# Context projections in fp16, and scores and maxima of an attention kernel moved to row tiles

## The reference

```
q = heads(xq @ wq);  k = heads(ctx @ wk);  v = heads(ctx @ wv)
q, k = rope(q), rope(k)                         # block 0 only
sim  = einsum('bhnd,bhmd->bhnm', q, k) * DH ** (-0.5)
a    = softmax(sim, axis=-1)
o    = einsum('bhnm,bhmd->bhnd', a, v)
out  = o.reshape(B, N, MID) @ wo + bo
```

## Time and profile before

| | |
|---|---|
| median of 3 runs | 6510.97 us |
| profiled execution | 6507.4 us, span 6505.6 us |
| TensorE matmuls busy | 5952.5 us (91%) |
| TensorE weight loads | 3685.3 us (57%) |
| VectorE busy | 4855.0 us (75%) |
| ScalarE busy | 4164.3 us (64%) |
| GpSimd busy | 2747.3 us (42%) |
| chain that ended last | PE 63%, DVE 14%, ACT 12%, issue 6% |

### The profile page before, as it was taken

How to read it: one execution, slowest core, us unless ns; L and a number is a source line. 1 busy time by engine, 2 the same in 40 slices (tenths; PEclk the granted TensorE clock), 3 DMA queues, 4 the chain that set the end, 5 groups by cost and what they waited for, 6 DMA issues and landing times.

```text
span 6505.6 us, 154557 instructions
## 1 busy us (share of the span) xinstructions
PE 5952.5 (91%) x58376; PEld 3685.3 (57%) x58376; DVE 4855.0 (75%) x9782; ACT 4164.3 (64%) x9234; POOL 2747.3 (42%) x2358
## 2 busy tenths in 40 slices
PE   6999989989899998998989999899897999989988
PEld 4566456754466645774456664577444665457744
DVE  6887777757788777775778877777578887877756
ACT  4556686657656668665755566766575566676656
POOL 3466126740256512674025651277302655127730
PEclk9999999989999999998999999999899999999989
DMA  3111011110111101111011110111001111011100
GB/s 88 37 34 27 22 37 31 33 28 13 51 35 33 30 21 37 33 30 28 17 47 37 34 27 20 39 32 33 24 19 50 30 32 30 18 41 31 28 20 12
DMA packets 347787, 206.23 MB, mean 32 GB/s; under 512 B 165005, under 2 KB 319981, under 8 KB 346926
## 3 DMA queue, kind: packets, MB, share of 16 engines
q1 hardware_dynamic: 347054, 196.34, 11.9%
HBM read 105.18 MB, written 1.05 MB: 16 GB/s over the span
## 4 chain that ended last, share of the span: by engine, by line
PE 63%; DVE 14%; ACT 12%; issue 6%; POOL 4%; SPq 1%; DVEq 0%; DMA 0%; ACTq 0%; POOLq 0%
PE ring L1354 32%; PE scores L1354 15%; PE o_acc L1354 15%; ACT qop L1652 5%; DVE max_part L2113 3%; POOL weight_sum L1316 2%; ACT region L1652 2%; DVE o_inv L2136 2%; ACT probs L1798 2%; DVE region L2075 2%; DVE ring L2089 1%; DVE ring L2092 1%; ACT qm L1652 1%; DVE raw L2087 1%; DVE qop L2072 1%
## 5 line engine op out<-in xcount | busy, mean ns | idle before, releaser
L2113 DVE TENSOR_REDUCE max_part<-ring 128x1 f32<-128x400 f32 (+2 forms) x4608 | 2425.0, 579 | 513.0 <-PE ring L1354 478.8
L1798 ACT ACTIVATE probs<-scores 128x512 f32<-128x512 f32 (+1 forms) x3840 | 2087.9, 599 | 954.2 <-PE scores L1354 929.5
L1316 POOL TENSOR_TENSOR weight_sum<-weight_sum,probs 128x512 f32<-128x512 f32 (+1 forms) x1408 | 1786.9, 1269 | 193.9 <-ACT probs L1798 60.1
L1354 PE MATMUL o_acc<-probs,region 128*32 128x256 f32 (+2 forms) x13312 | 1327.4, 383 | 11.4 <-ACT probs L1798 5.0
L1652 ACT ACTIVATE region<-ring 64x400 f16<-64x400 f32 (+4 forms) x1744 | 817.0, 479 | 463.5 <-PE ring L1354 374.1
L1316 POOL TENSOR_TENSOR weight_sum<-probs 128x512 f32<-128x512 f32 x256 | 324.8, 1269 | 1540.9 <-PE ring L1354 1096.8
L1354 PEld LDWEIGHTS o_acc<-probs,region 128*32 128x32 f32 (+2 forms) x13312 | 637.6, 123 | 400.9 <-ACT probs L1798 139.4
L1354 PE MATMUL scores<-qop,region 128*64 128x256 f16 (+1 forms) x6400 | 811.4, 274 | 21.4 <-ACT qop L1652 14.5
L1354 PE MATMUL scores<-qop,x_cop 128*64 128x256 f16 (+1 forms) x6400 | 805.2, 272 | 0.0
L1354 PE MATMUL ring<-nk,qm 128*128 128x400 f16 (+2 forms) x2560 | 709.0, 337 | 51.5 <-DVE max_part L2113 22.4
L1354 PE MATMUL scores<-qm,nk 128*128 128x512 f16 (+1 forms) x1920 | 656.0, 389 | 57.0 <-ACT probs L1798 31.4
(11 more groups left out here) (170 smaller groups left out, 7168.0 us busy)
## 6 DMA issues: line engine op xcount, KB each, us to landing
x_cop<-region SPq DMA_DIRECT2D x256, 200.1 KB, 3.1
stage<-in_wide SPq DMA_DIRECT2D x512, 64.0 KB, 1.9
nk<-region SPq DMA_DIRECT2D x192, 100.1 KB, 2.2
stage<-in_wide SPq DMA_DIRECT2D x128, 128.0 KB, 2.5
v_stage<-in_wide SPq DMA_DIRECT2D x256, 64.0 KB, 1.9
wo_stage<-in_wide SPq DMA_DIRECT2D x32, 512.0 KB, 3.9
cop_few<-kop_few SPq DMA_DIRECT2D x256, 32.0 KB, 1.9
ff_w<-in_ff_w SPq DMA_DIRECT2D x24, 256.0 KB, 3.3
```

The source lines that it names most:

```text
L1316: pool.tensor_tensor(total, before, probs[0:rows_, (un.chunk + k) % PROBS, :], ALU.add)\
L1354: return pe.matmul(out, lhs, rhs, start=start, stop=stop, skip_group_check=True)
L1798: act.activation(to, src, ACT.Exp, scale=t.scale).then_inc(exp_done.sem, 1)
L2113: dve.tensor_reduce(dst, src, AX.X, ALU.max).then_inc(*release(one))
```

## The change

It has three parts.

1. *Context in fp16.* The transposed context is stored as a high and a low fp16 part instead of fp32 (`ctx_t`, `src_t`), the low part by VectorE. The key and value weights of the wide cross stages are split the same way, times 32, at the start of the program: ScalarE makes the high, VectorE the low part, and a DMA stores them in device memory, from where each unit loads them. The narrow cross weights are folded and split once. A projection is then three fp16 products, high by high, high by low and low by high (`in_halves`), instead of one in fp32.
2. *Row tiles.* Operands stay in the order in which the projection leaves them: head h on its own 64 (wide) or 32 (narrow) partitions. A score or maximum of one head is a matmul whose weights have 64 or 32 rows and 128 columns. Heads write to different PSUM banks. The wide scores take four products for each head (high by high, high by low, low by high, and the shift). Maxima use the high parts alone, and no longer wait for the low part. The crossed copy, its DMAs, the masks and the DMAs of the narrow self stages are gone; narrow queries, and in self attention keys, are spread over the partitions by a small matmul (`spread`). Narrow cross keys are brought by twelve DMAs of 8 partitions for a unit instead of three of 32. All of an operand goes out of PSUM in one instruction of 128 partitions.
3. *One pool.* Scores and ring share seven banks, at most four for each use; scores are issued two banks at a time (2 heads by 2 key tiles).

The planner's table is changed with it, and its tile size is now a pair (rows, columns).

```diff
-RING, SLOTS, PROBS = 4, 3, 8
+POOL_BANKS, RING, SLOTS, PROBS = 7, 4, 4, 8
...
-            return [("max", (h, None), 0) for h in range(4)] + [("shift", 0, 0)]
-        out = [("max", (h, q), k) for g in (0, 2) for q in range(QT) for k in range(len(self.kc)) for h in (g, g + 1)]
-        return out + [("shift", 0, 0)]
+            return [("spread", 0, 0), ("spread", 1, 0)] + [("max", (h, None), 0) for h in range(4)] + [("shift", 0, 0)]
+        out = [("max", (h, q), k) for q in range(QT) for k in range(len(self.kc)) for h in range(4)]
+        return [("spread", 0, 0)] + out + [("shift", 0, 0)]
...
-def columns(what):
...
+def tile_of(what):
 
     if what[0] == "pre":
-        return P
+        return P, P
     un = CHUNKS[what[1]][0] if what[0] == "scores" else UNITS[what[1]]
-    if not un.t.wide:
-        return 32 if what[0] == "values" else P
-    if what[0] == "job" and un.t.jobs[what[2]][0] == "shift":
-        return P
-    return 64
+    side = 64 if un.t.wide else 32
+    if what[0] == "scores" or what[0] == "job" and un.t.jobs[what[2]][0] == "max":
+        return side, P
+    return P, side
...
-            deps = [("DVE", ("job", n, t.jobs.index(("low", k + 1, 0)))), ("DVE", ("job", n, t.jobs.index(("low", 0, 0))))]
-            self.part("PE", "max", due, one, 0.21 if t.cross else 0.3, deps, 0.2)
+            deps = [("ACT", ("job", n, op_job(t, k + 1))), ("ACT", ("job", n, op_job(t, 0)))]
+            self.part("PE", "max", due, one, 0.1 if t.cross else 0.16, deps, 0.25)
...
+        self.part("ACT", "split", due, one, 0.4, [])
+        self.part("DVE", "split", due, one, 0.55, [("ACT", one)])
+        self.part("SP", "split", due, one, 0.6, [("DVE", one)], 4.0)
...
-                        for block_, of_k, of_q in ((1, 0, 0), (2, 1, 0), (3, 0, 1)):
-                            to = slice(32 * block_, 32 * block_ + 32)
-                            sp.dma_start(nq[to, z, :], q[part, of_q, :]).then_inc(nq_in[z].sem, 16)
-                        for block_, of_k, of_q in ((1, 0, 0), (2, 1, 0), (3, 0, 1)):
-                            to = slice(32 * block_, 32 * block_ + 32)
-                            sp.dma_start(nk[to, z, 0:un.t.keys], k[part, of_k, 0:un.t.keys]).then_inc(nk_in[z].sem, 16)
+                            wait(taken(item_of(s, u, "keys", len(un.t.kc) - 1)))
+                        k = split_of(s, u, "keys")
+                        for h in range(4):
+                            rows_of = slice(32 * un.p + 8 * h, 32 * un.p + 8 * h + 8)
+                            for l, at in ((0, 8), (1, 16), (0, 24)):
+                                sp.dma_start(nk[32 * h + at:32 * h + at + 8, z, 0:un.t.keys], k[rows_of, l, 0:un.t.keys])\
+                                    .then_inc(nk_in[z].sem, 16)
...
+            wait((mod_full, 1))
+            for k, at in enumerate((SK, SV)):
+                sp.dma_start(kv_in[7][:, :, k, :], a["wide7"][:, 0:DC, at:at + P].rearrange("g p c -> p g c"))\
+                    .then_inc(kv_loaded[1], 16)
...
-                    pool.tensor_tensor(qm[:, un.narrow_at % QM_SLOTS, :, :], nq[:, z, :].unsqueeze(1).broadcast_to([P, 4, N]),
-                                       head_mask[:, :].unsqueeze(2).broadcast_to([P, 4, N]), ALU.mult)\
-                        .then_inc(masked.sem, 1)
...
+            def in_halves(out, lhs, rhs, product):
+
+                product(out, lhs[0], rhs[0], True, False)
+                product(out, lhs[0], rhs[1], False, False)
+                return product(out, lhs[1], rhs[0], False, True)
...
-                        last = mm_64(out[:, 0:w], stage[0:t.dk, w_at, k, W_K:W_K + P], src[0:t.dk, a0:a0 + w], True, True)
+                        if t.cross:
+                            halves = k_split_of(un)
+                            last = in_halves(out[:, 0:w], [halves[:, k, l, :] for l in range(2)],
+                                             [src[:, l, a0:a0 + w] for l in range(2)], mm_64)
...
-                            last = mm_64(out[:, m * w:(m + 1) * w], qop[:, z, h, qq * P:(qq + 1) * P],
-                                      kop_of(un)[:, h, a0:a0 + w], True, True)
+                            last = mm(out[:, m * w:(m + 1) * w], qop[part, z, 0, qq * P:(qq + 1) * P],
+                                      kop_of(un)[part, 0, a0:a0 + w], True, True)
...
-                    if g >= SLOTS:
-                        old, co = chunk_before(g, SLOTS)
-                        pe.wait_ge(exp_done.sem, exp_done.at(old.n, co + 1))
-                    r = t.rows(k)
-                    out = scores[0:r, g % SLOTS, :]
-                    if t.wide:
-                        for h in range(2):
-                            mm_64(out[:, h * N:(h + 1) * N], kop_of(un)[:, h, k * P:k * P + r], qop[:, z, h, :], True, False)
-                            last = mm_64(out[:, h * N:(h + 1) * N], cop_of(un)[:, h, k * P:k * P + r], qop[:, z, 2 + h, :],
-                                      False, True)
-                    else:
-                        last = mm(out, nk[:, un.narrow_at % NK_SLOTS, k * P:k * P + r],
-                                  qm[:, un.narrow_at % QM_SLOTS, 2 * half:2 * half + 2, :], True, True)
-                    last.then_inc(scores_full.sem, 1)
+                            pe.wait_ge(*taken(("job", n, op_job(t, t.ops - 1))))
+                    for one in (g, g + 1):
+                        pe.wait_ge(*room_for_scores(one))
+                    side, nz = P // t.heads, un.narrow_at % NK_SLOTS
+                    heads = [(c % t.heads + i, score_bank(g + i)) for i in range(2)]
+                    kop = kop_of(un)
+                    for m, k in enumerate(t.tiles(c // t.heads)):
+                        r = t.rows(k)
+                        at = slice(k * P, k * P + r)
+                        if t.wide:
+                            products = [(kop[:, 0, at], qop[:, z, 0, :]), (kop[:, 0, at], qop[:, z, 1, :]),
+                                        (kop[:, 1, at], qop[:, z, 0, :]), (shift_k[:, 0:r], shift_q[:, z, :])]
+                        else:
+                            products = [(nk[:, nz, at], nq_shift[:, nz, :])]
+                        for i, (keys, queries) in enumerate(products):
+                            for h, r_out in heads:
+                                part = slice(side * h, side * h + side)
+                                last = mm(ring[0:r, r_out, m * N:(m + 1) * N], keys[part], queries[part],
+                                          i == 0, i == len(products) - 1)
+                    last.then_inc(scores_full.sem, 2)
...
-                        part = slice(64 * h, 64 * h + 64)
-                        if i == 0:
-                            for to in (slice(0, 64), slice(64, 128)):
-                                last = copy(qop[to, z, h, :], ring[part, bank(one), 0:N])
-                        else:
-                            a0, w = t.kc[i - 1]
-                            last = copy(kop_of(un)[part, h, a0:a0 + w], ring[part, bank(one), 0:w])
-                    last.then_inc(op_high.sem, 1)
+                    high, w = operand(un, i, 0)
+                    copy(high, ring[:, bank(one), 0:w]).then_inc(op_high.sem, 1)
...
+                def split_high_weights(i):
+                    s, g = SPLITS[i]
+                    if g == 0:
+                        act.wait_ge(kv_loaded[s // 7], 48 if s == 1 else 32)
+                    copy(kv_out[s][:, g, :, 0, :], kv_in[s][:, g, :, :], scale=GAIN).then_inc(kv_high, 1)
...
+                def context_low(one, j):
+
+                    _, s, u, m = one
+                    a0 = (j % 4) * BANK
+                    w = min(BANK, M - a0)
+                    to = (ctx_t if j < 4 else src_t)[:, u % 2, :, a0:a0 + w]
+                    dve.wait_ge(ctx_high.sem, ctx_high.at((s, u), j + 1 if j < 4 else 2 * j - 2))
+                    dve.tensor_tensor(to[:, 1, :], ring[0:DC, bank(one), 0:w], to[:, 0, :], ALU.subtract).then_inc(*release(one))
...
-                    kop, v = kop_of(un), ring[:, bank(made), :]
                     dve.wait_ge(op_high.sem, op_high.at(n, i + 1))
-                    for h in range(2):
-                        part, other = slice(64 * h, 64 * h + 64), slice(64 - 64 * h, 128 - 64 * h)
-                        if i == 0:
-                            last = dve.tensor_tensor(qop[part, z, 2 + h, :], v[part, 0:N], qop[part, z, h, :], ALU.subtract)
-                        else:
-                            a0, w = t.kc[i - 1]
-                            last = dve.tensor_tensor(kop[other, h, a0:a0 + w], v[part, 0:w], kop[part, h, a0:a0 + w],
-                                                     ALU.subtract)
-                    last.then_inc(*release(made))
+                    high, w = operand(un, i, 0)
+                    dve.tensor_tensor(operand(un, i, 1)[0], ring[:, bank(made), 0:w], high, ALU.subtract).then_inc(*release(made))
```

481 lines of the change are left out of this document (301 added, 180 removed).

## The result

The changed kernel takes 6238.83 us (median of 4 runs, 6222.14 to 6249.06), the kernel before beside it 6511.69: a ratio of 0.9577 (95% interval 0.9561 to 0.9593). Forecast were 6000 us, so the gain is 273 us instead of 511. The profiled execution took 6242.82 us, its span is 6241.0.

The account below looks back on a forecast made before the run. TensorE streaming bounds the wide cross stages; in narrow cross stages three engines wait in turn. Terms 4 x (-20 - 17 - 66 - 28) + 12 = -512 took 6507.4 us to 5995, say 6000; range 5790 to 6330.

Parts of the forecast that it names:

- wide stages: Wide cross stages: shorter by 20 us (rope stage) and 17 us per pair, from TensorE's stream and fewer stalls.
- context values in fp16: Wide cross value projections: three fp16 steps take 0.21 us per key tile against 0.22, no gain; better bound -11 us a stage.
- change of tile: TensorE in wide cross units: more changes of tile size at 0.10 us each, adding 23 and 15 us a stage.
- Rivals A: Score and maximum matmuls: row tiles do not run side by side; about 7080 us, 4% chance.
- B: TensorE: a change between row and column tiles costs more than 0.10 us; at 0.3, 6930 us; 6% chance.
- C: Wide cross stages: short fp16 products cost 0.11 us each and maxima find no overlap; about 6290 us, 15% chance.
- Overlap of the maxima: Wide cross units: neighbouring maxima of different heads run side by side, -12 and -15 us a stage; lower bound of gain 0.
- stalls: Wide cross stages: a third of TensorE's stalls of 35 and 25 us goes, -11 and -7 us.
- Self stages: Self attention per pair: stage 6 -11, stage 0 -6, stages 3 and 9 -5 and -6; together -28 us.
- The start: Program start: sixteen weight splits on ScalarE delay the first query copy from 35.14 to near 53 us; +12 us once.
- Narrow cross: Narrow cross stages: TensorE falls to 122 us, VectorE bounds at some 90% busy; 160 and 167 us, -33 each per pair.
- rival D: Narrow cross stages: engines keep waiting in turn, -11 instead of -33 us a stage; 6176 us, 15% chance.

Follow-up runs that it names:

- kernel with two products: Changed kernel with the last of the three fp16 products left out in the wide cross key and value projections; 6051.15 us, 0.9289 of before.
- experiments 1 to 3: Changed kernel with added narrow cross matmuls (6217.9, 6197.3, 6244.0 us); with masked full-array narrow scores and maxima (6216.89, 6301.89); with those over 128 rows, unmasked (6143.15).
- kernel with whole rows: Changed kernel, same order and copies, with narrow cross scores and maxima over all 128 rows instead of 32, head mask left out; 6143.15 us, 0.9434 of before.

## Why the prediction was right and wrong

*The sum.* The time lies within the forecast's range of 5790 to 6330 us, and that is partly luck. Over the four pairs the wide cross stages gave -244 us (forecast -148), the self stages with the start -158 (forecast -100), and the narrow cross stages +134 (forecast -264). With the first two as forecast, the failed third would have put the kernel near 6390, outside.

*Direction and wide stages: right, and short.* Forecast were -20 and -17 us, measured -30 and -31. The step that was mis-sized is *context values in fp16*: 0.21 us per key tile from the one row of short matmuls, measured 0.17. That is -11 us of streaming a stage, the better bound, and makes up most of the difference, though not all: in the kernel with two products 0.72 of what the stream lost came back as time. The price of a product (0.51), of scores (0.44 a key tile) and of a change of tile (0.10) came as reckoned, as did their number: about 350 and 260 changes in these stages against 130 and 120. Rivals A, B and C fall with it. Overlap of the maxima is seen, but not how often, so its -12 and -15, and the -11 and -7 for stalls, aren't told apart.

*Self stages: right, and short.* -28 was forecast per pair; stage 0 gave 23 (mean of the last three pairs), stage 6 18 and stages 3 and 9 together 2. For stage 0 -6 was forecast. VectorE's work there fell by 13 us (121.8 to 108.8), so it was not VectorE alone: that a fifth bank takes 10 us more off says that banks for jobs hold this stage too. Stages 3 and 9, forecast at -11, gained almost nothing: their clock fell as well, to 0.77 and 0.76 from 0.95 and 0.81.

*The start: the size was right, the cause was not.* I blamed ScalarE's splits; taking them away changes nothing. The first stage 0 is 55.6 us longer than the next, before 43.2: +12 (against the mean of the later three +17). By the time the splits end (56.7) a DMA would hold TensorE as long (57.0).

*Narrow cross: wrong.* This is the step that failed, 264 us of the sum: "VectorE should be some 90% busy: 160 and 167 us, -33 and -33". Measured are +17 and +16, so 213 and 215 us over the four pairs. By the forecast's own sign, above 180 us, this part is wrong; VectorE is busy for 68 and 73% of these stages in the second pair, not 90. The forecast took TensorE's stream down from 163 to 122 us and the clock as given, at 0.97. The stream fell further still, as a key tile of four heads takes 0.11. It was this lighter work that cost the clock, as experiments 1 to 3 show. An estimate: 881 - 106 = 775 us more at the lower level at 0.30 us each are some 236 us, or 29 a stage. Without them the stages would hold 1469 us, 13 a stage less than before, 184 instead of 213; by the kernel with whole rows less 15 a stage it is 187. So rival D (182 and 189 us) had about the size at the full clock; no rival had the clock. The full-clock stretches show the forecast's mechanism all the same, with VectorE back to back and 2.57 us for two key tiles; but the first units of each item, with norms and FFN in between, do not reach it.

Could it have been seen? The trace before had the hint: 0.97 and 0.96 in the narrow cross stages of the second pair are 10 and 17 us at 1.2 GHz, where the wide cross ones have 7 and 3 in twice the time, and a clock of 0.81 in stage 9, where TensorE works least. A term "TensorE does less, and may be granted less" was missing. The Trainium skill, TensorE: Matmul & The Clock Gate, A second HAM failure mode: psum-queue depth-cycling, describes the clock falling and coming back where TensorE idles briefly between groups of matmuls. The trace agrees as far as it goes: in the second pair TensorE waits over 0.15 us 47 and 49 times in these stages, 23 us in each (before 19 and 23 times, 7 and 9 us), and each is cut into 12 stretches at alternating levels of the clock, before into 3 and 7. No run here changes the waits alone. The same page of the Trainium skill, Terms, puts the penalty of a stretch at half its length at the lower clock; these units show 0.30. Part of that time was waiting before, 0.24 and 0.40 us of the 2.57 above.

## What to carry to other kernels

Where TensorE isn't the bound, a faster form for its matmuls can be a loss: look at the granted clock stage by stage before and after, and price a us at the lower level from two units at the same place (here 0.30). Work added to an in-order engine to hold its clock up paid here only where a wait, or the matmuls of other row tiles beside it, hid it. To judge one form of matmul, change that alone and keep order, copies and waits. And when a forecast comes in, compare it term by term: here two terms that gave more hid part of the failure of a third.

## What the runs showed of the hardware

- With order, copies and waits equal, narrow cross stages ran at 0.97 with matmuls over 128 rows, one after another, and at 0.67 to 0.84 with 32 rows, up to four at a time side by side; 8 of the latter (256 columns) streamed in 0.23 us.
- Added matmuls in tiles of 32 rows raised the granted clock too: 881 us at 1.2 GHz in stages 4 and 10 became 389.
- Executions of one kernel differ by their clock: the kernel with two products ranged from 5999.8 to 6084.2 us with mean clocks of 0.914 and 0.895, that is 84 us for 245 us more at 1.2 GHz, 0.34 each. In which stages they differ isn't shown.
- Matmuls in different tiles of 32 rows start within 0.01 us of each other, also when they belong to different products (a filler and two scores at 3794.89).
- Short fp16 matmuls of 128 columns by 64, in column pairs with a weight load each, take 0.056 us a pair: 24 of them in 0.67 us.
